# The Y product of the next unit put into the block that forms the lower inverse of this one, on four 32x32 tiles, for three units of four

## The reference: what is computed

```python
def step(state, inp):
    q_t, k_t, v_t, g_t, b_t = inp
    state = state * jnp.exp(g_t)[..., None, None]
    corr = jnp.einsum('bhk,bhkv->bhv', k_t, state)
    v_new = (v_t - corr) * b_t[..., None]
    state = state + jnp.einsum('bhk,bhv->bhkv', k_t, v_new)
    o_t = jnp.einsum('bhk,bhkv->bhv', q_t, state)
    return (state, o_t)
```

## Time and profile before

| | |
|---|---|
| runs (3) | 1138.3, 1139.51, 1141.66 us; median 1139.51 |
| profiled execution | 1139.21 us, span from first to last instruction 1136.7 us |
| granted TensorE clock, mean | 0.990 of full speed |
| PE busy | 1080.6 us (95%) in 11676 matmul instructions |
| PEld busy | 752.4 us (66%) |
| DVE busy | 849.2 us (75%) |
| ACT busy | 694.5 us (61%) |
| POOL busy | 471.5 us (41%) |
| chain that ended last | PE 59%, DVE 15%, issue 9%, POOL 7%, ACT 5%, DMA 3% |

### The profile page before, as it was taken

How to read it: one execution, slowest core, us unless ns; L and a number is a source line. 1 busy time by engine, 2 the same in 40 slices (tenths; PEclk the granted TensorE clock), 3 DMA queues, 4 the chain that set the end, 5 groups by cost and what they waited for, 6 DMA issues and landing times.

```text
span 1136.7 us, 29246 instructions
## 1 busy us (share of the span) xinstructions
PE 1080.6 (95%) x11676; PEld 752.4 (66%) x11676; DVE 849.2 (75%) x1445; ACT 694.5 (61%) x1243; POOL 471.5 (41%) x688
## 2 busy tenths in 40 slices
PE   8979899999999999999998889889999999999998
PEld 3444455555555565555555556679999989999987
DVE  5989778879879778779777745687767776767662
ACT  5778577777677776777867756643443344434434
POOL 1649475584683882873976712210100000001100
PEclk9999899999999999999999999999999999999999
DMA  4223335656656666666556532431122122111100
GB/s 133 54 65 86 92 64 98 115 120 115 125 116 93 142 140 142 129 129 118 76 81 204 147 129 76 140 85 48 49 52 54 52 61 65 48 48 48 29 21 14
DMA packets 168214, 102.36 MB, mean 90 GB/s; under 512 B 98416, under 2 KB 148720, under 8 KB 167184
## 3 DMA queue, kind: packets, MB, share of 16 engines
q1 hardware_dynamic: 166928, 100.30, 39.8%
q10 hardware_dynamic: 1152, 0.21, 0.1%
HBM read 63.24 MB, written 14.67 MB: 69 GB/s over the span
## 4 chain that ended last, share of the span: by engine, by line
PE 59%; DVE 15%; issue 9%; POOL 7%; ACT 5%; DMA 3%; SPq 2%; ACTq 0%; DVEq 0%; POOLq 0%
PE proj L593 13%; DVE conv L1223 6%; PE out L1803 5%; PE turned_v_chain L1803 5%; PE proj L1872 5%; PE turned_v_chain L1884 4%; PE proj L1742 4%; PE gram L608 3%; POOL inverse L1501 3%; PE gram L1777 2%; POOL rank_one L1498 2%; DMA vg_weights<-in_vg_w 1%; PE proj L1791 1%; PE turned_v_chain L599 1%; PE out L617 1%
## 5 line engine op out<-in xcount | busy, mean ns | idle before, releaser
L1223 DVE SCALAR_TENSOR_TENSOR conv<-proj,kq_weights,conv 128x504 f32<-128x504 f32 (+2 forms) x261 | 189.2, 729 | 66.5 <-ACT conv L932 61.0
L593 PE MATMUL proj<-xT,vg_weights 128*128 128x512 f32 x384 | 193.9, 629 | 4.7 <-DMA vg_weights<-in_vg_w 3.0
L2136 POOL TENSOR_TENSOR rope<-rope_part,rope_part 128x512 f32<-128x512 f32 x32 | 40.1, 1275 | 315.6 <-DVE rope_part L2058 315.6
L593 PE MATMUL proj<-xT,kq_weights 128*128 128x512 f32 x348 | 166.7, 605 | 3.4 <-DVE conv L1223 2.9
L1223 DVE SCALAR_TENSOR_TENSOR conv<-proj,vg_weights,conv 128x504 f32<-128x504 f32 (+2 forms) x192 | 139.5, 727 | 25.1 <-ACT conv L932 22.0
L1501 POOL TENSOR_TENSOR inverse<-inverse,rank_one 128x30 f32<-128x30 f32 (+14 forms) x240 | 133.9, 558 | 18.8
L1498 POOL TENSOR_TENSOR rank_one<-inverse 128x30 f32<-128x30 f32 (+14 forms) x240 | 119.1, 496 | 21.0 <-DVE inverse L1284 6.0
L593 PEld LDWEIGHTS proj<-xT,kq_weights 128*128 128x128 f32 x348 | 62.2, 189 | 78.0 <-issue 61.4
L593 PEld LDWEIGHTS proj<-xT,vg_weights 128*128 128x128 f32 x384 | 66.5, 192 | 58.8 <-issue 49.9
L608 PEld LDWEIGHTS gram<-keys_q 128*64 128x64 f32 x896 | 56.8, 136 | 42.5 <-issue 25.7
L943 ACT ACTIVATE keys_q<-conv 128x512 f32<-128x512 f32 x96 | 63.5, 663 | 32.4 <-DVE conv L1223 31.2
(11 more groups left out here) (271 smaller groups left out, 2358.2 us busy)
## 6 DMA issues: line engine op xcount, KB each, us to landing
kq_weights<-in_kq_w SPq DMA_DIRECT2D x32, 390.0 KB, 6.6
vg_weights<-in_vg_w SPq DMA_DIRECT2D x32, 390.0 KB, 6.8
o_scratch<-oT SPq DMA_DIRECT2D x32, 256.0 KB, 2.2
o_in<-o_scratch SPq DMA_DIRECT2D x16, 512.0 KB, 4.2
o_rs<-o_rs_quarters SPq DMA_DIRECT2D x88, 64.0 KB, 6.3
diagonal<-gram_decayed SPq DMA_DIRECT2D x128, 32.0 KB, 1.9
inverse<-inverse SPq DMA_DIRECT2D x32, 128.0 KB, 3.0
q_first<-rope SPq DMA_DIRECT2D x128, 32.0 KB, 1.9
```

The lines of the kernel that those rows point to most:

```text
L593: mm = e.matmul(bank(c, u)[:], w[:, (k * 3 + c % 3) * 128:(k * 3 + c % 3 + 1) * 128], xT[g][:, k, :], start=(k == 0), stop=(k == KD - 1))
L1223: e.scalar_tensor_tensor(acc(c, u)[:, :, back:], src[:, :, 0:S - back], weights(c, u)[:, j:j + 1], acc(c, u)[:, :, back:], ALU.mult, ALU.a ...
L2136: e.tensor_tensor(turned[half][:].rearrange("p b r q -> p r b q"), parts[2 * half][:], parts[2 * half + 1][:], op).then_inc(s_turned, 1)
```

## The change

Before, Y of every unit was a block of its own on two tiles of the array (rows 0, 64 to columns 32, 96) at the start of the unit's round. Now only part 0 of a batch has this block. For parts 1 to 3, Y(u+1) is formed in the same block as the lower inverse of unit u, matmul by matmul in turn: the sixteen of Y now write partition rows 0 to 31 and 64 to 95 of `CH` (tiles 0,0 and 64,64), those of the lower inverse rows 32 to 63 and 96 to 127 (tiles 32,32 and 96,96). The copy of Y(u+1) moves: on ACT it stands behind `copy_inverse_low(u)` (rounds 10 to 32), on DVE behind the convolution of V0 (later rounds). The copy now crosses from partition rows i-1 to i. Since Y(u+1) then stands where the lower result goes, the chain's high block of unit u also waits for that copy (`y_copied`). No instruction is added or dropped.

```diff
@@ tensor
+                def y_step(u, b, i):
+                    return e.matmul(CH[rows(i), b * RB:(b + 1) * RB], gE[u % LAG][rows(i), b, rows(i + 1)],
+                                    D32[rows(i), GB * part(u) + b, :], start=True, stop=True)
...
                 def chain_inverse_low(u):
                     if part(u) == 0:
                         e.wait_ge(s_solve, SOLVE * batch(u) + TURNED2)
+                    else:
+                        chain_free(u)
                     e.wait_ge(s_yout, 2 * (u + 1))
                     for b in range(GB):
                         for i in (0, 2):
+                            if y_ahead(u + 1):
+                                y = y_step(u + 1, b, i)
                             mm = e.matmul(CH[rows(i + 1), 256 + b * RB:256 + (b + 1) * RB],
                                           D32T[rows(i + 1), GB * part(u) + b, :], Y[rows(i + 1), b, :], start=True, stop=True)
                     mm.then_inc(s_d10, 1)
+                    if y_ahead(u + 1):
+                        y.then_inc(s_y, 1)
+
+                def y_copied(u):
+                    if y_ahead(u + 1):
+                        e.wait_ge(s_yout, 2 * (u + 2))
...
                     e.wait_ge(s_d10out, 2 * (u + 1))
+                    y_copied(u)
...
-                    y_later = live(uc) and s > U and part(uc) == 0
-                    if live(uc) and not y_later:
+                    y_now = y_first(uc)
+                    if y_now and s <= U:
                         chain_y(uc)
@@ scalar
                     for i in (1, 3):
-                        e.activation(Y[rows(i), :, :], CH[rows(i), 0:256].rearrange("p (b c) -> p b c", c=RB),
+                        e.activation(Y[rows(i), :, :], CH[rows(i - 1), 0:256].rearrange("p (b c) -> p b c", c=RB),
...
-                    if Y_BY_ACT and live(uc) and s <= U:
+                    if y_first(uc) and s <= U:
                         copy_y(uc)
...
                     if live(uc):
                         copy_inverse_low(uc)
+                    if y_ahead(uc + 1) and s <= U:
+                        copy_y(uc + 1)
                     if live(ud):
                         copy_v(0, ud)
@@ vector
-                    if live(uc) and s > LAG and not (Y_BY_ACT and woven):
+                    if y_first(uc) and s > U:
                         copy_y(uc)
...
                     elif live(uc):
                         convolve(V0, uc)
+                    if y_ahead(uc + 1) and s > U:
+                        copy_y(uc + 1)
```

More of the change, by code:

```diff
@@ L135 @@
 ROWS_SLOT = 5
-Y_BY_ACT = True
 POOL_STEPS = 3 + 14 + 4
@@ L304, in delta_phase @@
         low_later = lambda u: joined(u + 1)
+        y_ahead = lambda u: live(u) and part(u) != 0
+        y_first = lambda u: live(u) and part(u) == 0
         high_chain = EB[:].rearrange("p (b s) -> p b s", b=GB)
@@ L691, in tensor, with chain_free @@
                     gram(1, ub)
-                def chain_y(u):
-                    if part(u) == 0:
-                        e.wait_ge(s_solve, SOLVE * batch(u) + TURNED)
+                def chain_free(u):
                     if low_later(u - 1):
@@ L699, in chain_y @@
                         e.wait_ge(s_wloout, u)
+                def y_step(u, b, i):
+                    return e.matmul(CH[rows(i), b * RB:(b + 1) * RB], gE[u % LAG][rows(i), b, rows(i + 1)],
+                                    D32[rows(i), GB * part(u) + b, :], start=True, stop=True)
+                def chain_y(u):
+                    e.wait_ge(s_solve, SOLVE * batch(u) + TURNED)
+                    chain_free(u)
                     if u == 0:
@@ L703, in chain_y @@
                         for i in (0, 2):
-                            mm = e.matmul(CH[rows(i + 1), b * RB:(b + 1) * RB], gE[u % LAG][rows(i), b, rows(i + 1)],
-                                          D32[rows(i), GB * part(u) + b, :], start=True, stop=True)
+                            mm = y_step(u, b, i)
                     mm.then_inc(s_y, 1)
@@ L815, in tensor @@
                         project(V0, uc)
-                    if y_later:
+                    if y_now and s > U:
                         chain_y(uc)
@@ L1075, in scalar @@
                 copy_inverse_low(0)
+                copy_y(1)
                 copy_w_high(0)
@@ L1311, in copy_y @@
                     for i in (1, 3):
-                        e.tensor_copy(Y[rows(i), :, :], CH[rows(i), 0:256].rearrange("p (b c) -> p b c", c=RB)).then_inc(s_yout, 1)
+                        e.tensor_copy(Y[rows(i), :, :], CH[rows(i - 1), 0:256].rearrange("p (b c) -> p b c", c=RB)).then_inc(s_yout, 1)
                 def add_q_squares(u):
```

## The result

The changed kernel takes 1143.54 us in the median of 15 runs (1140.2 to 1146.35), the kernel before 1139.39 us in the median of 15 (1136.96 to 1145.72). The ratio is 1.0032 with a 95% interval of 1.0017 to 1.0047: slower by 3.7 us by the ratio, where a median of 1139.0, no change, was forecast. The profiled execution took 1145.91 us (span 1143.4), 2.4 above the median, so its losses are larger than those of a usual run.

The account below looks back on a forecast made before the run. PE was taken to bound the rounds up to 590 us, with ACT just in time. Steady 0.0, start +0.3 and late units -0.8 gave -0.5 us: 1138.7 like the profiled execution, median 1139.0, range for 8 in 10 1134.5 to 1144.

Parts of the forecast that it names:

- Y blocks that go, 18 x 0.62: Rounds of units 1 to 23: 18 Y blocks of parts 1 to 3 leave PE, 0.62 us each, 11.2 us saved.
- Merged block, +0.01: Lower inverse with Y on four tiles: 0.01 us more a block, 0.2 over 17 blocks; about 0.63 us long.
- rival (b): Merged block's four tiles run two at a time: +0.62 us a block, 0.2 us in all, same verdict; chance 0.12.
- rival c: Merged block's four tiles take turns: +1.2 us a block, 1147 us and more; chance 0.04.
- Copies give 0.80 back in parts 1 and 2, 0.58 in part 0: ACT's Y copies delay V's copy; PE idles ahead of the second V transposes: 9.6 us over 12 rounds, 2.9 in part 0.
- steady sum of 0: Rounds 10 to 32: savings and costs come to +1.5 us, old PE waits absorb 1.5, leaving 0.0, bounds -2.2 and +1.5.
- Start, +0.3: Unit 0's high chain waits for the copy of Y(1), unit 1 loses its block: +0.3 us, between -0.62 and +0.80.
- Late units, -0.8: Units 25 on: -3.7 us for six blocks, +0.2, +2.7 for high chains awaiting DVE's copy; bounds -3.5 and +4.6.
- The clock, +-1.3 and not in the sum: A stretch at 1.2 instead of 2.4 GHz behind idle PE costs 1.3 us; may come or go, counted only in the range.
- Rival (d): Every late high chain waits for DVE's copy behind a convolution: late units +4.6 us, 1144.4 or 1145.9 us; chance 0.12.

Follow-up runs that it names:

- e1_early: Changed kernel with the change for units 1 to 23 only; units 24 to 31 form Y in their own block: 1.0001 of the kernel before (0.9987 to 1.0016).
- e2_late: Kernel before with the change for units 25 and on only, copies on DVE: 1.0032 of the kernel before (1.0014 to 1.0050).
- e18_only30: Kernel before with the change for the Y of unit 30 alone: 1140.98 against 1139.0 us, 1.0015 (0.9999 to 1.0030).
- e7_two_later: Changed kernel with Y's copy behind V's on ACT and Y's matmuls in one piece behind the lower inverse's: 1142.12 us, 1.0013 of the kernel before.

## Why the prediction was wrong

- **Y blocks that go, 18 x 0.62**: right, and part 3's rounds show it (-0.6).
- **Merged block, +0.01**: too low. It costs 0.05 to 0.23 more than 0.63, some 2 us over 17 blocks. It went into the wait behind it, as rival (b) had it for a larger price. Four turns (rival c) would have been 1.8 us or more, and no block took over 0.90. Gotcha 1 of the Trainium skill's "TensorEngine Tiling (Array Packing)" says that different row tiles can't access one PSUM bank at the same time. The trace disagrees for these four tiles, which differ in their columns as well as in their rows.
- **Copies give 0.80 back in parts 1 and 2, 0.58 in part 0**: right. Rounds of +0.17 and -0.6 were forecast and are there, and so is the idle time ahead of `turn_v(1)`. It is 9.4 and not 12 us, and the longer merged block takes part of the difference. The steady sum of 0 is confirmed by `e1_early`.
- **Start, +0.3**: it was -0.4 at unit 1, too little to matter.
- **Late units, -0.8: this is the step that failed**, by some 4.5 us: the late units alone measured +3.7 (`e2_late`, 1.0032). I counted 0.62 us for each of six Y blocks as won, less the waits of the high chain. Three parts were wrong. In units 26 and 27 PE isn't the bound: POOL's scan is, up to unit 27's output, and blocks taken out of PE's stream are worth nothing there (the prediction rests on no row of POOL there). The copies on DVE were priced only at the high chain, not at what stands behind them on DVE: `oT` and with it the load of `x_in` stand 1.0 us further behind the convolution. And the waits had a price of their own, in the clock.
- **The clock, +-1.3 and not in the sum**: mis-sized. The fall behind 2.19 us of waiting cost 3.2 us of longer matmuls, 2.4 after what an old wait took up, and 1.8 more in the next round. 13 of 15 runs of the changed kernel have a mean clock of 0.986 or less, against 31 of 140 before. Filling that wait takes 2 to 3 us off. Which wait makes the clock fall in a given run stays open.
- **Rival (d)**: its mechanism is there with its size, in one unit and not in six: 1.32 us in unit 29, where 1.35 was worked out. I had given it two units. With what follows it, `e18_only30` puts it near 2 us (1.0015, 0.9999 to 1.0030).

So the steady rounds came out by the mechanism that was forecast, and the late ones did not. The time, 1143.54, lies inside 1134.5 to 1144 only because the range was wide; the change of +0.32% is real and has the other sign than the forecast -0.5 us.

## What to carry to other kernels

Before a block taken out of one engine's stream is counted as won, look in that stretch for the wait ahead of it and what ends it: a saving in front of a wait for another engine only lengthens the wait. A longer idle stretch of PE may cost more than nothing, as the matmuls behind it can run at the lower clock; a few idle repeats of work there can pay, as they did here where PE waited 2.2 us and not where it waited 1.6. When a copy goes onto another engine, look at everything that this engine does behind it, not only at who waits for the copy. And when a copy is moved, place it behind what PE waits for next: here one place further on, and on the engine that has room, turned a loss of 0.3% into a gain of 0.3%.

## What the runs showed of the hardware

- Four 32x32 tiles that write one PSUM bank, each with its own rows and its own columns of the array, overlap: 64 instructions in 0.68 to 0.86 us (0.90 once), against 1.04 for the same work two tiles at a time and 0.62 for half of it.
- Two blocks of 32x32 tiles right behind each other, on different tiles, cost 0.51 + 0.53 us (`e7_two_later`), 0.1 less each than such a block between blocks of other tile shapes (0.62).
- Ahead of unit 27's output the granted clock fell behind 2.2 us of idle PE in two profiles (changed, `e2_late`) and not in five others with 2.18 to 2.22; it fell behind 1.64 us in one (`e1_early`) and not in five others with 1.63 or 1.64. So it is a matter of the execution, and the median moves by how often it happens: single profiles of two kernels can differ by falls that have nothing to do with the change, as at 764 us here.
